# The last three turns of a decoder block's attention written out as one order per engine

## The reference

```python
x = x + attn(layernorm(x))                 # 16 heads of 32, rotary, causal softmax
x = x + xattn(layernorm(x), ctx, pos, pos) # 32 heads of 16, axial rotary, ctx has 256 features
x = x + ffn(layernorm(x))                  # silu(z @ Wg.T) * (z @ Wu.T) @ Wd.T, 1408 hidden
# in ffn: W = (wq - 128) * scale per row, wq integers
```

## Time and profile before

| | us |
|---|---|
| runs: median (lowest to highest) of 3 | 1717.02 (1715.77 to 1717.54) |
| the profiled execution | 1716.51 |
| its span, first to last instruction | 1714.7 |
| PE, PEld busy | 1643.8, 1292.9 |
| DVE, ACT, POOL busy | 1169.4, 977.7, 488.2 |
| mean granted TensorE clock | 0.986 |

### The profile page before, as it was taken

The page is one execution under the profiler, slowest core; times in us unless marked ns, Lnnn a source line. Parts: engine busy times, 40 slices in busy tenths (PEclk is TensorE's granted clock), DMA queues, the critical chain, the costliest instruction groups (busy, mean ns, idle before and its releaser), DMA issues. The chain is left out here.

```text
span 1714.7 us, 40656 instructions
## 1 busy us (share of the span) xinstructions
PE 1643.8 (96%) x14656; PEld 1292.9 (75%) x14656; DVE 1169.4 (68%) x2111; ACT 977.7 (57%) x3824; POOL 488.2 (28%) x473
## 2 busy tenths in 40 slices
PE   5899999999999999999999999985999999999997
PEld 4677777777777777777777777764788888888885
DVE  7678887887888887887888888765644434444332
ACT  5567776776777776777767767764532222222221
POOL 4233443334333343334433343321010111011011
PEclk9999999999999999999999999988999999999999
DMA  5000101111110011011010011020620220220110
GB/s 210 29 31 31 36 29 53 29 29 36 38 44 29 29 36 53 29 29 36 30 53 29 29 36 39 8 78 15 219 74 1 73 73 0 73 73 3 71 50 25
DMA packets 55097, 80.98 MB, mean 47 GB/s; under 512 B 4880, under 2 KB 25488, under 8 KB 55056
## 3 DMA queue, kind: packets, MB, share of 16 engines
q1 hardware_dynamic: 55056, 80.43, 14.4%
HBM read 63.63 MB, written 16.78 MB: 47 GB/s over the span
## 5 line engine op out<-in xcount | busy, mean ns | idle before, releaser
L715 ACT ACTIVATE prob<-bank,nmax 128x128 f32<-128x128 f32 x1536 | 542.9, 407 | 177.1 <-DVE nmax L891 177.1
L715 ACT ACTIVATION_READ_ACCUMULATOR prob<-bank,nmax 128x1 f32 x1536 | 378.4, 246 | 0.0
L891 DVE TENSOR_REDUCE nmax<-bank 128x4 f32<-128x512 f32 x384 | 238.5, 684 | 80.2 <-PE bank L502 71.9
L1215 PE MATMUL fbank<-shared,piece_hi 128*128 128x512 f32 x1152 | 280.3, 394 | 0.0
L1215 PEld LDWEIGHTS fbank<-shared,piece_hi 128*128 128x128 f32 x1152 | 215.8, 187 | 53.1
L393 POOL TENSOR_TENSOR rope_buf<-rope_buf 128x512 f32<-128x512 f32 x128 | 167.2, 1306 | 185.7 <-DVE rope_buf L848 185.6
L478 PE MATMUL bank<-shared,z1T_h 128*128 128x512 f32 x768 | 203.2, 406 | 4.3 <-ACT shared L698 2.6
L1367 DVE SCALAR_TENSOR_TENSOR h<-fbank,su_c,sil 128x512 f32<-128x512 f32 x88 | 66.0, 750 | 206.5 <-PE fbank L1215 198.8
L478 PEld LDWEIGHTS bank<-shared,z1T_h 128*128 128x128 f32 x768 | 140.3, 189 | 41.5 <-issue 8.9
L1301 ACT ACTIVATE sil<-fbank,sg_c 128x512 f32<-128x512 f32 x88 | 60.6, 689 | 174.9 <-PE fbank L1215 172.0
L1307 ACT ACTIVATE h_h<-h 128x512 fp32r<-128x512 f32 x88 | 55.8, 634 | 175.7 <-DVE h L1367 175.7
(11 more groups left out here) (157 smaller groups left out, 2930.1 us busy)
## 6 DMA issues: line engine op xcount, KB each, us to landing
xA<-in_x SPq DMA_DIRECT2D x32, 256.0 KB, 2.9
xB<-in_x SPq DMA_DIRECT2D x32, 256.0 KB, 2.8
x_scratch<-x SPq DMA_DIRECT2D x32, 256.0 KB, 2.0
shared_loaded<-x_scratch SPq DMA_DIRECT2D x8, 1024.0 KB, 7.7
xr<-x_scratch SPq DMA_DIRECT2D x8, 1024.0 KB, 5.6
out<-xr SPq DMA_DIRECT2D x8, 1024.0 KB, 4.3
cx<-in_ctx SPq DMA_DIRECT2D x32, 128.0 KB, 2.2
range_window<-in_wg SPq DMA_DIRECT2D x27, 112.0 KB, 2.0
```

The source lines that it names most:

```text
L715: last = nc.scalar.activation(prob[:, c, i, :], S[c][:, i * P:(i + 1) * P], ACT.Exp, bias=nmax[:, c, i:i + 1], accum_out=rs[:, h:h + 1])
L891: nc.vector.tensor_reduce(out=nmax[:, c, :], in_=S[c][:, :].rearrange("p (g k) -> p g k", g=G), op=ALU.max, axis=AX, negate=True).then_inc ...
L1215: last = nc.tensor.matmul(dst[:, :], w[:, k, cols], z[:, k, :], start=(n == 0), stop=(n == len(passes) * KT - 1))
```

## The change

The last three turns are no longer calls of `turn`. Each engine gets a function `last()` with its whole order. Token L's cross-attention no longer follows that of M as a turn of its own: L's z2 comes early, its q2 product lies between M's two halves, and its scores follow as soon as M's second half has left the banks. The second half of L's probabilities is handled bank by bank (`transpose_bank`, `copy_bank`, `maxima_of_bank`, scores for one bank at a time, `s_done` counted per bank). L's contexts go to PC instead of PB, so that M's output product can stand in PB. The head of the feed-forward part is cut in pieces: statistics in two pairs, one weight piece's high part at a time, the flag early, the transposes of z behind L's last attention and into the four S banks. The three pieces' low parts move into the second program. SP loads L's context and residual ahead of the feed-forward head, not behind it.

```diff
-        def schedule(turn, fori, before_last=None, after_last=None):
+        L, M, N = B - 1, B - 2, B - 3
+        def schedule(turn, fori, last):
...
             turn(B - 2, B - 3, B - 1, None, B - 4)
-            if before_last is not None:
-                before_last()
-            turn(B - 1, B - 2, None, None, B - 3)
-            turn(None, B - 1, None, None, B - 2)
-            if after_last is not None:
-                after_last()
-            turn(None, None, None, None, B - 1)
+            last()
```

SP:

```diff
+            def last():
+                sp.wait_ge(cxT_lo, L)
+                sp.dma_start(cx[:, :, :], ctx_in[L, :, :, :]).then_inc(cx_in, 16)
+                sp.wait_ge(x1_r, L)
+                sp.dma_start(xB[:, :], x[L, :, :]).then_inc(xb_in, 16)
+                load_ffn_head()
+                for q in (N, M, L):
+                    sp.wait_ge(x2_r, q + 1)
+                    sp.dma_start(x2_dram[q, :, :], x2[:, :]).then_inc(x2_out, 16)
```

GpSimd:

```diff
+            def last():
+                ctx_low(2, N)
+                rope_sum("q2", M)
+                spread(1, L, rinv1, rbc1, H1, DK1)
+                split_ctx(L)
+                add_bias(M)
+                ctx_low(1, L)
+                rope_sum("k2", L)
+                rough_rstd(2, L)
+                rope_sum("q2", L)
+                spread(2, M, rinv2, rbc2, H2, DK2)
+                pool.wait_ge(f_ve, 1)
+                pool.tensor_tensor(fr0[:, :], fve[:, :], mhalf_c[:, :], ALU.pow).then_inc(f_rs, 1)
+                ctx_low(2, M)
+                spread(2, L, rinv2, rbc2, H2, DK2)
+                add_bias(L)
+                ctx_low(2, L)
```

TensorE, from the self-attention of L on:

```diff
+            def last():
...
+                attend1()
+                pe.wait_ge(v2_r, M + 1)
+                transpose_reciprocals(1, L)
+                pe.wait_ge(rT_r["q2"], M + 1)
+                pe.wait_ge(rT_r["k2"], M + 1)
+                scores2("2a")
+                pe.wait_ge(cxT_lo, L + 1)
+                project(PA, cxT_h, cxT_l, "kv2", CKT, slice(0, D)).then_inc(pj["k2"], 1)
+                pe.wait_ge(cn_r[1], L + 1)
+                project(PC, cn_h, cn_l, "o1", KT, lo_ready=(cn_lo[1], L + 1)).then_inc(pj["o1"], 1)
...
+                collect("2a", M)
+                scores2("2b")
+                project_q2(L)
+                pe.wait_ge(x2_r, N + 1)
+                attend2("2a")
+                pe.wait_ge(zT_lo[2], L + 1)
+                project(PC, cxT_h, cxT_l, "kv2", CKT, slice(D, 2 * D)).then_inc(pj["v2"], 1)
+                transpose_prob("2b", M)
+                transpose_q2(L)
+                collect("2b", M)
+                pe.wait_ge(rT_r["q2"], L + 1)
+                pe.wait_ge(rT_r["k2"], L + 1)
+                scores2("2a")
+                attend2("2b")
+                transpose_reciprocals(2, M)
+                transpose_bank("2a", L, 0)
+                transpose_bank("2a", L, 1)
+                for c in range(G):
+                    pe.wait_ge((pTe_r, pTo_r)[c % 2][2], 2 * nth("2a", L) + c // 2 + 1)
+                    scores2("2b", (c,))
+                    if c + 2 < G:
+                        transpose_bank("2a", L, c + 2)
+                pe.wait_ge(v2_r, L + 1)
+                attend2("2a", PC)
+                transpose_bank("2b", L, 0)
+                project_o2(M)
+                for c in (1, 2, 3):
+                    transpose_bank("2b", L, c)
+                collect("2b", L)
+                attend2("2b", PC)
+                pe.wait_ge(riT_r[2], M + 1)
+                transpose_reciprocals(2, L)
+                transpose_ffn_head()
...
+                project_o2(L)
```

VectorE, at the head of the second program:

```diff
+            for n in range(HEAD):
+                nc.vector.scalar_tensor_tensor(out=lo[n], in0=ffn["raw"][n], scalar=ZERO_POINT, in1=hi[n],
+                                               op0=ALU.subtract, op1=ALU.subtract).then_inc(w_lo, 1)
```

More of the change, by code:

```diff
@@ L360, in load_ffn_head @@
                     sp.dma_start(ffn["raw"][n], ffn["source"][n]).then_inc(f_w[n], 16)
-            schedule(turn, sp.Fori, before_last=load_ffn_head)
+            schedule(turn, sp.Fori, last)
         @block.gpsimd
@@ L435, in turn @@
                 if cq is not None:
[L436 to L438 removed]
+                    add_bias(cq)
                 if sq is not None:
@@ L455, in _ @@
             pool.wait_ge(c_in, 32)
-            schedule(turn, pool.Fori)
+            schedule(turn, pool.Fori, last)
         @block.tensor
@@ L689, in _ @@
             transpose_z1(0)
-            schedule(turn, pe.Fori)
+            schedule(turn, pe.Fori, last)
         @block.scalar
@@ L789, in _ @@
             split_high(LATE[:2])
-            def split_ffn_head():
-                for n in range(HEAD):
-                    act.wait_ge(f_w[n], 16)
-                    nc.scalar.activation(ffn["hi"][n], ffn["raw"][n], ACT.Copy, bias=-ZERO_POINT).then_inc(f_hi, 1)
-            schedule(turn, act.Fori, after_last=split_ffn_head)
+            schedule(turn, act.Fori, last)
         @block.vector
@@ new lines, in maxima_of_bank, with last @@
+            def maxima_of_bank(u, q, c):
+                dve.wait_ge(s_done[kind(u)], nth(u, q) + c + 1)
+                nc.vector.tensor_reduce(out=nmax[:, c, :], in_=S[c][:, :].rearrange("p (g k) -> p g k", g=G),
+                                        op=ALU.max, axis=AX, negate=True).then_inc(nmax_r[kind(u)], 1)
+            def last():
+                reduce_windows()
+                row_maxima("1", L, range(G))
+                context2(N, PB)
+                rope("q2", M, PA, DK2, *axial(M), DK2 ** -0.5)
+                ffn_statistics((0, 1))
+                add_cross(N)
+                row_sums(L)
+                even_copies("1", L)
+                ffn_statistics((2, 3))
+                context1(L)
+                row_maxima("2a", M, (0, 1))
+                rope("k2", L, PA, DK2, *axial(L), 1.0)
+                row_maxima("2a", M, (2, 3))
+                add_self(L)
+                dve.wait_ge(x1_r, L + 1)
+                statistics(2, x1A, L)
+                normalise(2, x1A, z2, L)
+                even_copies("2a", M)
+                dve.wait_ge(zT_hi[2], L + 1)
+                low(z2T_l, PC[:, :], z2T_h, zT_lo[2])
+                row_maxima("2b", M, range(G))
+                rope("q2", L, PA, DK2, *axial(L), DK2 ** -0.5)
+                key_pairs(L)
+                ffn_aggregate()
+                even_copies("2b", M)
+                row_sums2(M)
+                raise_flag()
+                row_maxima("2a", L, range(G))
+                copy_bank("2a", L, 0)
+                context2(M, PB)
+                for c in (1, 2, 3):
+                    copy_bank("2a", L, c)
+                    maxima_of_bank("2b", L, c - 1)
+                maxima_of_bank("2b", L, 3)
+                ffn_normalise()
+                row_sums2(L)
+                copy_bank("2b", L, 0)
+                add_cross(M)
+                copy_bank("2b", L, 2)
+                context2(L, PC)
+                for k in range(KT):
+                    dve.wait_ge(f_zTh, k + 1)
+                    nc.vector.tensor_tensor(ffn["zT_l"][:, k, :], FZ[k][:, :], ffn["zT_h"][:, k, :], ALU.subtract).then_inc(f_zTl, 1)
+                add_cross(L)
@@ L957, in turn @@
                     even_copies("1", sq)
-                if has_c and not has_s:
-                    ffn_statistics()
                 if has_c:
@@ L991, in turn @@
                     normalise(2, x1A, z2, sq)
-                if has_c and not has_s:
-                    ffn_normalise()
                 if is_first(cq):
@@ L1079, in split_ffn_head @@
                 nc.vector.tensor_scalar(ffn["low_flag"][:, :], rng_max[:, :], EXACT, None, ALU.is_gt).then_inc(rng_flag, 1)
[L1080 to L1083 removed]
             dve.sem_inc(rng_r, 1)
[L1086 removed]
+            schedule(turn, turns_of, last)
             dve.wait_ge(rng_flag, 1)
@@ L1239, in program @@
             def program(nb, nx, first, low):
-                w_split = w_lo if low else w_hi
+                w_split, head = (w_lo, 0) if low else (w_hi, HEAD)
                 wait(pe, zT_hr, KT * nb)
```

211 lines of the change are left out of this document (144 added, 67 removed).

## The result

| | before | changed |
|---|---|---|
| median, us | 1716.39 (1715.58 to 1717.54, 4 runs) | 1700.17 (1699.93 to 1700.37, 4 runs) |
| the profiled execution | 1716.51 | 1700.37 |
| its span | 1714.7 | 1698.5 |
| PE busy, mean granted clock | 1643.8, 0.986 | 1642.9, 0.992 |

The ratio is 0.9906, with a 95% interval of 0.9894 to 0.9919: 16.2 us faster, where 18.5 were forecast. Three stretches make up the difference of the two profiled executions. The one up to the scores of L's self-attention is 1.4 shorter (1117.86 to 1116.42) though the change touches nothing there: the low-clock stretches of the first 100 us fell differently. The last turns take 64.9 instead of 79.2, 14.2 less (1116.42 to 1181.36, the end of the last x2), where the walk had 60.6 with its allowance for the clock.

What follows compares the result with a forecast made beforehand. One dependent chain through M's, then L's attention, set by engine order, bound the last 79 us. The walk ended at 1177.0, plus 1.5 for the clock 1178.5, 18.5 before 1197.0: forecast 1698.5 us, range 1696.5 to 1703.5.

Steps and rivals of the forecast that it cites:

- the walk: New engine order followed along its dependent chain with old durations, ending at 1177.0, or 1178.5 with clock allowance; chance 0.80.
- x1 of L: L's x1 add comes at 1137.1 instead of 1139.73, since context and reciprocals precede the scores; 2.6 us gained.
- z2 of L: L's normalisation directly follows its x1, no longer behind maxima, rotary passes and GpSimd's sum; gain so far 8.6 us.
- Scores of L: Scores of L's first half start at 1152.4 instead of 1162.79, after M's second half; gain so far 10.4 us.
- the product's cover: L's q2 product lies from 1144 to 1147 under M's exponentials, costing nothing; without that cover, 2.9 us.
- The second half of L: L's banks interleave with exponentials without a gap, ending at 1166.7 instead of 1182.0; gain so far 15.3 us.
- The clock: Allowance for low clock after TensorE's stops: 1.5 us, a third of the old 5, with ends 0 and 5.
- line 827: Small 128x1 step before z2 of L, taken as 0.16 without GpSimd's port lock; 0.9 us later if stalled.
- The end: From the last attention's start at 1169.4 to the last x2: 7.5 us instead of 8.8, ending at 1177.0.
- At nothing: Three low parts (4.02) moved into VectorE's idle time, 3.6 left; x2's load and the flag also costed at nothing.
- orders that hold each other up: Rival: L's banks don't interleave, the 5.6 gap mostly returns; 8 less gained, 1706; 0.15 together with no overlap.
- The clock at 1.2 GHz "for good": Rival: TensorE at 1.2 GHz from 1133 on gives 1720.5 to 1721, slower by 4; 0.03 with similar losses.

Runs made afterwards that it cites:

- e4_port: Changed kernel with one more 128x512 GpSimd addition right behind the power in L's normalisation; 1702.42 us, one execution.
- e8_z2_late: Changed kernel with VectorE's copies and maxima for M's second half back ahead of L's statistics and z2, other engines in step; 1710.70 us.
- e7_q2_late: Changed kernel with L's q2 product back behind the second half of M's transposes; 1710.60 us.
- e3_fill: Changed kernel with 24 idle transposes in TensorE's two stops before the first and second bank of L's probabilities; 1698.11 us.
- e2_whole: Changed kernel with scores of L's second half made for all four banks at once, behind all four transposes; 1700.07 us.
- c_changed: Changed kernel again, unaltered, run beside three later variants on one chip; 1701.92 us.
- e9_fill_M_too: Changed kernel with idle transposes in TensorE's two stops before L's second half (24) and in M's first-half stop (12); 1698.76 us.
- e10_split_o2: As e9_fill_M_too, with the last four matmuls of M's output product moved behind L's last transposes; 1697.46 us.

## Why the prediction was right, and where it was off

The sign, the place and the size of the gain were right: 16.2 of 18.5. A part of how near it came was luck, since 1.4 of the 16.2 came from the untouched start; the last turns themselves gave 14.2. The bullet on the sum says where the rest went.

- *x1 of L, 2.6.* Forecast for 1137.1, which is 1135.7 with the 1.4 of the start taken off; it starts at 1135.75.
- *z2 of L, 8.6 in all.* z starts at 1138.99; 1140.4 less 1.4 is 1139.0. e4_port puts the small step at 0.77, where 0.9 was priced, and e8_z2_late shows that most of the rest hangs on this place.
- *Scores of L, 10.4.* 34.8 behind the start, forecast 34.5. This is the profile in which M's part kept full clock; six others of the same order have 35.6 to 36.4. e7_q2_late shows that the product's cover was real; I priced its loss at 2.9, and it is worth some 10, with what the clock adds.
- *The second half of L, the step that failed.* I gave it no gap and a bank's scores no price of their own; the only row was the eight-matmul group at 1.15, and a quarter of it, 0.3, would leave TensorE free enough to keep ScalarE fed. They take 1.15 each and 2.07 at the lower level, where the gaps add up to 3.0. At full clock this hardly shows in the exponentials (they run from 1155.7 to 1168.3 in e3_fill, 12.6 against 12.2 in the walk), but M's output product then ends 1.6 past them, not 0.5. These are 0.4 and 1.1; two hand-overs each 0.1 shorter than in the walk leave the 1.3 by which 18.3 exceeds its 17.0.
- *The clock, 1.5, mis-sized.* It cost 4.3 in this half alone. I took a third of the old loss by the length of stops. The stops were even shorter than I had them, 1.77 at most, and the clock fell all the same; and it met the one stretch in which TensorE was bound, where 10 us at half the clock, some 5 us of work, came out at the end as 4.3. The range of 0 to 5 had it. The upper end of my forecast for this case, 3.5 more "for the clock and line 827", is the clock's part alone; with the 0.9 of line 827 it is 4.4.
- *The end.* 7.5 from the last attention to the last x2, as forecast.
- *The sum.* The two errors, 5.6 less the 1.5 allowed and 0.3 before, make 4.4 late; the start gave back 1.4 and the feed-forward part 0.5, and 2.4 are missing of what was forecast for the profiled execution.
- *At nothing.* The low parts, the load and the flag cost nothing; the first h comes 5.9 behind the last x2 (7.6 before). The margin for the low parts was 1.6, though, and not the 3.6 that I counted, since the first h itself now comes sooner.

Of the rivals, "orders that hold each other up" was half right: the gap between the halves did not return, but 3.0 us of gaps appeared inside the second, by TensorE and not by VectorE's passes. And that the gap is gone is worth less than I thought: with it back, e2_whole is no slower, so of the gain none is shown to come from the order by banks at the low clock. The clock at 1.2 GHz "for good" did not come: it was low for about 10 us, from 1158.8 on, and recovered while TensorE was busy, as it had before the change. By the Trainium skill's "TensorE: Matmul & The Clock Gate", section "HAM oscillation — how this bites in real kernels", bursts between waits lose the full clock again and again; here it was lost once in these 65 us, and twice in the profile of c_changed.

## What to carry to other kernels

Where two dependent chains share five engines, walk the new order row by row before believing a sum of busy times: the two moves that look small on their own (a product under someone else's exponentials, a normalisation ahead of someone else's maxima) each carried some 10 of 16 us. When work is cut into pieces so that it can interleave, price a piece from a row of a piece, never as a fraction of the whole. And price a low clock by where it falls: where TensorE set the pace, some 5 us of work lost to it came out as 4.3 at the end; in M's part in e3_fill some 3.4 us made L's scores 1.5 later.

## What the runs showed of the hardware

Calls to several groups run beside each other, and what one group has to do is done in a row. In this kernel each group of rows always writes the same bank, so no run tells whether it is the group or the bank that takes its work in a row. The Trainium skill's "TensorE: Matmul & The Clock Gate", section "Why this matters for your kernels", says that matmuls of small depth in distinct groups of 32 rows run concurrently; these rows agree.

The clock fell without a stop. In e9_fill_M_too and e10_split_o2 TensorE waited for nothing from 1152.6 to 1168, and the granted clock went to 0.50 at about 1161.9 and 1163.2 all the same, for some 3.4 us, in or just behind the scores of the last two banks. In e3_fill the same order kept full clock. With the stops filled the part from L's scores to the last attention took 18.3, 19.9 and 19.0, against 22.6 in both profiles of the changed kernel; with M's stop filled, L's scores came at 34.8 in three profiles of three, and without it in one of seven. So in these profiles filled stops went with later, shorter falls or none, but did not exclude one. What triggers it these runs don't settle. Nor do they settle why the changed kernel varied over 0.4 us in one set of runs and over 4.2 in another; in those runs the slower an execution, the lower its mean clock (1700.35 at 0.991, 1704.57 at 0.988).
